# Splitting layer outputs before they are turned, and turning them by DMA: a four-layer graph network on one core

## The reference

```
x = layernorm(x + L0(x));  x = layernorm(x + L1(x));  x = layernorm(x + L2(x));  out = layernorm(x + L3(x))
L0: h = layer_norm(relu(conv(x, W1, b1)), gamma, beta);  conv(h, W2, b2) + x
    conv(x, W, b) = D^-1 H B^-1 H^T (x W^T) + b,  H = (adj != 0), D and B sums over H and the first row of adj
L1: q, k = split(x @ Wqk);  v = x @ Wv
    w = mask * sum(q * (adj @ (k * mask)), features) / 16
    softmax(w over the 64 nodes of a graph) * v
L2: 8 heads of 32: softmax((q k^T / sqrt(32)) * 2 adj) v, then Wo
L3: xg = x * sigmoid(deg * Wd + bd);  s = sigmoid(xg Wqk^T + b);  a = (s s^T / 16) * adj, rows divided by their sums
    relu(a @ xg @ Wl^T + bl + xg @ Wr^T)
```

## Time and profile before

| | us |
|---|---|
| three runs | 959.28, 960.44, 968.0 (median 960.44) |
| span of the profiled execution (first to last instruction) | 966.0 |
| PE / DVE / ACT / POOL busy | 887.1 / 742.3 / 724.6 / 670.3 |
| share of the 16 DMA engines | about 41% |
| pace of a step with all streams live | about 26.5 |

### The profile page before, as it was taken

The page is one execution under the profiler, slowest core; times in us unless marked ns, Lnnn a source line. Parts: engine busy times, 40 slices in busy tenths (PEclk is TensorE's granted clock), DMA queues, the critical chain, the costliest instruction groups (busy, mean ns, idle before and its releaser), DMA issues.

```text
span 966.0 us, 34322 instructions
## 1 busy us (share of the span) xinstructions
PE 887.1 (92%) x12124; PEld 761.5 (79%) x12124; DVE 742.3 (77%) x2292; ACT 724.6 (75%) x1740; POOL 670.3 (69%) x1005
## 2 busy tenths in 40 slices
PE   4778898999999999999999999999999999988674
PEld 3556677888888888888888888888888888876542
DVE  5556776888888888888888888888888888876632
...
PEclk9798899999999999999999999999999999999955
...
GB/s 207 20 21 83 111 100 65 119 111 106 112 123 121 116 116 102 103 112 109 106 109 110 122 123 117 114 106 99 111 119 103 104 115 116 109 97 116 97 48 22
DMA packets 194573, 99.46 MB, mean 103 GB/s; under 512 B 112866, under 2 KB 194276, under 8 KB 194532
## 3 DMA queue, kind: packets, MB, share of 16 engines
...
...
## 4 chain that ended last, share of the span: by engine, by line
PE 53%; ACT 11%; POOL 10%; DVE 10%; issue 9%; DMA 5%; SPq 1%; POOLq 0%; DVEq 0%; ACTq 0%
PE bank L537 12%; PE bank L539 12%; PE bank L538 12%; POOL rFl L1375 3%; PE bank L562 3%; ACT r L886 3%; PE bank L754 2%; PE bank L815 2%; DMA k_by_head<-kst 2%; DMA Ks<-k_by_head 2%; PE bank L650 1%; ACT x L846 1%; PE bank L682 1%; ACT rFh L826 1%; POOL rsC L1391 1%
## 5 line engine op out<-in xcount | busy, mean ns | idle before, releaser
L1375 POOL TENSOR_TENSOR rFl<-r,rFh 128x512 f16<-128x512 f32 x64 | 74.2, 1160 | 81.1 <-ACT rFh L826 81.1
L537 PE MATMUL bank<-z1h,W 128*128 128x256 f16 x256 | 71.9, 281 | 6.3 <-DVE z1l L1025 6.3
L538 PE MATMUL bank<-z1l,W 128*128 128x256 f16 x256 | 71.8, 281 | 0.0
L537 PE MATMUL bank<-W,rFh 128*128 128x256 f16 x256 | 71.8, 280 | 0.0
L539 PE MATMUL bank<-z1h,W 128*128 128x256 f16 x256 | 71.7, 280 | 0.0
L539 PE MATMUL bank<-W,rFl 128*128 128x256 f16 x256 | 71.7, 280 | 0.0
L538 PE MATMUL bank<-W,rFh 128*128 128x256 f16 x256 | 71.7, 280 | 0.0
L1476 POOL TENSOR_TENSOR late<-late,Smx 128x512 f32<-128x512 f32 x64 | 66.8, 1043 | 1.3 <-DVE Smx L1282 1.0
L1375 POOL TENSOR_TENSOR y0l<-y,y0h 128x512 f16<-128x512 f32 x32 | 37.3, 1166 | 42.3 <-ACT y0h L826 42.3
L870 ACT ACTIVATE Pf<-bank,Dinv 128x128 f32<-128x128 f32 x64 | 20.0, 363 | 49.7 <-DVE Dinv L1167 49.7
L886 ACT ACTIVATE r<-bank,b1c 128x256 f32<-128x256 f32 x128 | 50.1, 471 | 4.8 <-PE bank L539 4.8
...
## 6 DMA issues: line engine op xcount, KB each, us to landing
Qs<-q_by_head SPq DMA_DIRECT2D x96, 128.0 KB, 2.7
Ks<-k_by_head SPq DMA_DIRECT2D x96, 128.0 KB, 3.2
Vbd<-vst SPq DMA_DIRECT2D x128, 66.0 KB, 2.1
xin<-x SPq DMA_DIRECT2D x32, 256.0 KB, 2.8
q_by_head<-qst SPq DMA_DIRECT2D x32, 256.0 KB, 2.5
k_by_head<-kst SPq DMA_DIRECT2D x32, 256.0 KB, 2.1
out<-late SPq DMA_DIRECT2D x32, 256.0 KB, 2.9
...
```

The source lines that it names most:

```text
L537: pe.matmul(o, sh, mh, start=start, stop=False, skip_group_check=True)
L538: pe.matmul(o, sh, ml, start=False, stop=False, skip_group_check=True)
L1375: return pool.tensor_tensor(dst, a, b, ALU.subtract)
```

## The change

- **Split before turning.** `x1`, `x2`, `cx`, `xg` and the convolution matrix are cast and subtracted in node-major order into one float16 tile with a high and a low half (`x1s`, `x2s`, `cxs`, `xgs`, `Ps`), and one DMA transpose on SP turns both halves (`x1T`, `x2T`, `cxT`, `xgT`, `Pt`). The PE transposes of these tiles go away. The low parts of `x1` and `cx` are made by POOL, those of `x2`, `xg` and `Ps` by DVE.
- **Layer 1's maximum over a scratch.** The logits `wcol` are written to DRAM (`w_by_node`, a column of single floats) and read back so that each partition has the 64 logits of its graph (`wrow`); DVE takes the maximum of that. Both PE transposes of the logits go away; the sum of the exponentials becomes two float16 matmuls.
- **Two normalizations on VectorE.** `x1` and the output `x4` are made by `tensor_scalar` (subtract, multiply) on DVE, no longer by ACT; POOL's `nb` goes away. The product that makes `xg` moves from POOL to DVE, and ACT's `g2` goes away.
- **Queries stacked later.** `park_q` and `fetch_q` move from `stream2` to `stream3`, one step later.
- Loads: adjacency arrives in the layouts that the tiles need, so `atA`, `aC` and `atG` are one DMA each in place of two, three and two.
- All order tables are new.

```diff
+            def turn(dst, src, done):
+                return sp.dma_start_transpose(dst, src).then_inc(ev(done), 16)
+            def turn_x2(at):
+                sp.wait_ge(ev("x2_lo"), at.n()).then_inc(ev("sp_held"), 1)
+                if at.earlier(1):
+                    sp.wait_ge(ev("v"), at.n(-1)).then_inc(ev("sp_held"), 1)
+                turn(x2T[:].rearrange("p t l c k -> p (t l c) k"), x2s[:].rearrange("p t l d -> p (t l d)"), "x2_turned")
...
+            def park_w(at):
+                sp.wait_ge(ev("w_masked"), at.n()).then_inc(ev("sp_held"), 1)
+                sp.dma_start(w_by_node[at.par].rearrange("t p -> p t"), wcol[:], allow_slow_non_contiguous=True).then_inc(ev("w_parked"), 16)
+            def fetch_w(at):
+                sp.wait_ge(ev("w_parked"), at.chain(16, 16)).then_inc(ev("sp_held"), 1)
+                for b in range(2):
+                    rows = slice(b * NODES, (b + 1) * NODES)
+                    sp.dma_start(wrow[rows], w_by_node[at.par][:, rows].rearrange("(o t) k -> o t k", o=1).broadcast_to(
+                        [NODES, TILES, NODES])).then_inc(ev("w_spread"), 16)
...
             def stream1(at):
-                return
+                turn_x1(at)
                 yield
             def stream2(at):
+                park_w(at)
+                yield
+                fetch_w(at)
+                yield
+                turn_x2(at)
+                yield
+                load_layer2(at)
+                yield
+            def stream3(at):
                 park_q(at)
                 yield
                 fetch_q(at)
                 yield
-                load_layer2(at)
-                yield
-            def stream3(at):
                 park_k(at)
...
             def stream2(at):                                   # PE
-                pe.wait_ge(ev("w_masked"), at.n())
-                pe.transpose(bC[:, 0:P], wpad[:], ident[:]).then_inc(ev("w_turned"), 1)
-                yield
-                pe.wait_ge(ev("w_shifted"), at.n()).then_inc(ev("pe_held"), 1)
-                pe.transpose(bC[:, D:D + P], wrm[:].rearrange("t b k -> t (b k)"), ident[:]).then_inc(ev("w_back"), 1)
...
-                pe.wait_ge(ev("xC"), at.n())
+                pe.wait_ge(ev("x2_turned"), at.chain(16, 16))
                 if at.earlier(1):
                     pe.wait_ge(ev("s_masked"), at.tile(1, -1))
-                turn(bD0, x2).then_inc(ev("x2_turned"), 1)
-                yield
-                first_needs(at, 5)
-                pe.wait_ge(ev("x2F_lo"), at.n())
-                project_fm(bD1, Wq, x2Fh, x2Fl).then_inc(ev("q"), 1)
+                project_turned(bD1, Wq, x2T).then_inc(ev("q"), 1)
...
-                act.wait_ge(ev("x2_turned"), at.n())           # ACT
-                cast(x2Fh[:].rearrange("p c k -> p (c k)"), bD0[:]).then_inc(ev("x2F_hi"), 1)
+                act.wait_ge(ev("xC"), at.n())
+                cast(x2s[:, :, 0], x2[:]).then_inc(ev("x2_hi"), 1)
...
+            def norm(k, dst, at):                              # DVE, for x1 and x4
+                dve.wait_ge(ev("rstd" + k), at.chain(2, 2))
+                for t in range(TILES):
+                    m = dve.tensor_scalar(dst[:, t], pre[k][:, t], mv[k][:, t, 0:1], rs[k][:, t:t + 1], ALU.subtract,
+                                          ALU.mult)
...
-                dve.wait_ge(ev("w_turned"), at.n())
-                dve.tensor_reduce(wmx[:], wv, AX.X, ALU.max).then_inc(ev("c_softmax"), 1)
+                dve.wait_ge(ev("w_spread"), at.chain(32, 32))
+                dve.tensor_reduce(wmx[:], wrow[:], AX.X, ALU.max).then_inc(ev("c_softmax"), 1)
...
-                low(x2Fl[:].rearrange("p c k -> p (c k)"), bD0[:], x2Fh[:].rearrange("p c k -> p (c k)")
-                    ).then_inc(ev("x2F_lo"), 1)
+                dve.tensor_tensor(x2s[:, :, 1], x2[:], x2s[:, :, 0], ALU.subtract).then_inc(ev("x2_lo"), 1)
```

More of the change, by code:

```diff
@@ L84, in build @@
         q_by_head = [nc.dram_tensor(f"q_by_head{i}", (2, P, 2 * TOK), F16).ap() for i in range(2)]
+        w_by_node = [nc.dram_tensor(f"w_by_node{i}", (TILES, P), F32).ap() for i in range(2)]
         k_by_head = [nc.dram_tensor(f"k_by_head{i}", (2, P, 2 * TOK), F16).ap() for i in range(2)]
@@ L372, in load_layer1 @@
                 sp.dma_start(aC[:, at.par], at_group(adj_mask, at)).then_inc(ev(f"C_in{at.par}"), 16)
-                for b in range(2):
-                    sp.dma_start(mrow[64 * b:64 * b + 64, at.par], mr[b, bass.ds(at.group(), 1)].broadcast_to(
-                        [64, TILES, NODES])).then_inc(ev(f"C_in{at.par}"), 16)
             def load_layer2(at):
@@ L385, in load_layer3 @@
                     sp.wait_ge(ev("attn"), at.n(-2)).then_inc(ev("sp_held"), 1)
[L386 to L389 removed]
+                sp.dma_start(atG[:, at.par], at_group(adj_graph, at)).then_inc(ev(f"atG_in{at.par}"), 16)
+            def turn(dst, src, done):
+                return sp.dma_start_transpose(dst, src).then_inc(ev(done), 16)
@@ L616, in stream0 @@
                 yield
-                pe.wait_ge(ev("p_f"), at.n())
-                for t in range(TILES):
-                    m = pe.transpose(bA[:, TOK + t * P:TOK + (t + 1) * P], Pf[:, t], ident[:])
-                m.then_inc(ev("p_turned0"), 1)
-                yield
-                pe.wait_ge(ev("p_lo"), at.n())
+                pe.wait_ge(ev("p_turned"), at.chain(16, 16))
                 pe.wait_ge(ev("x_lo"), at.n())
@@ L976, in stream4 @@
                 yield
-                act.wait_ge(ev("cx_turned"), at.n())
-                cast(cFh[:].rearrange("p c k -> p (c k)"), bF0[:]).then_inc(ev("cF_hi"), 1)
+                act.wait_ge(ev("cx"), at.tile(1))
+                if at.earlier(1):
+                    act.wait_ge(ev("cx_turned"), at.chain(16, 16, -1))
+                cast(cxs[:, :, 0], cx).then_inc(ev("cx_hi"), 1)
                 yield
@@ L1169, in stream0 @@
                 dve.wait_ge(ev("p_hi"), at.n())
-                low(Pl[:, at.par].rearrange("p t k -> p (t k)"), bA[:, TOK:2 * TOK],
-                    Ph[:, at.par].rearrange("p t k -> p (t k)")).then_inc(ev("p_lo"), 1)
+                for t in range(TILES):
+                    m = low(Ps[:, t, 1], bA[:, t * P:(t + 1) * P], Ps[:, t, 0], Dinv[:, t:t + 1])
+                m.then_inc(ev("p_lo"), 1)
                 yield
@@ L1377, in rstd @@
             def rstd(k, at):
-                per = 2 if k in CENTRED else 3
                 eps, factor = {"F": (EPS, 1.0 / (WS * WS)), "G": (EPS * WS * WS, 1.0)}.get(k, (EPS, 1.0))
@@ L1389, in rstd @@
                 yield
-                pool.wait_ge(ev("rstd" + k), at.chain(per, 1))
+                pool.wait_ge(ev("rstd" + k), at.chain(2, 1))
                 pool.tensor_tensor(rs[k][:], ve[k][:], powm[:], ALU.pow).then_inc(ev("rstd" + k), 1)
-                if k in CENTRED:
-                    return
-                yield
-                pool.wait_ge(ev("rstd" + k), at.chain(3, 2)).then_inc(ev("pool_held"), 1)
-                for t in range(TILES):
-                    m = pool.tensor_scalar(nb[k][:, t:t + 1], mv[k][:, t, 0:1], rs[k][:, t:t + 1], -1.0, ALU.mult,
-                                           ALU.mult)
-                m.then_inc(ev("rstd" + k), 1)
             def bias_tm(dst, src, b):
```

338 lines of the change are left out of this document (178 added, 160 removed).

## The result

The changed kernel takes 1358.0 us (median of 4 runs, 1355.5 to 1364.9) beside 959.9 of the kernel before on the same chip: ratio 1.415 [1.407, 1.424], so 398 us slower. The forecast was 988 us, its range 928 to 1042.

A forecast was written before the change was run, and what follows sets the result against it. PE set the pace before; afterwards a loop through SP's transpose of `x2` was to make steps 27.0 us against 26.5. 966.0 + 13 (steps) + 15 (filling, draining) = 994, less 5.6 for the profiled run: 988 us, range 928 to 1042.

The forecast's parts named there:

- What closes the step: Loop through SP's transpose of `x2` and the logits' round trip: (a), (b), 0.1 and (c) make 27.0 us a step.
- (a): Logits' round trip through DRAM, `w_by_node` write (landing 2.1, at most 3.2) and `wrow` reads: 5.45 us.
- (b): DVE's work from `wmx` to `x2_lo`: 10.4 us without waits, 10.9 with one wait for the keys.
- (c): SP's issues and gaps from the transpose of `x2` to the next `w_by_node`: 10.5 us.
- The second loop: From keys landing at 12.85 us through scores, first-layer products, ACT, squares and DVE up to the logits: 27.1 us.
- DVE and POOL: Work per step after the change: DVE about 23.2 us, POOL about 20.5, neither over PE's 23.2.
- Filling and draining: Pipe's start and end, one group 16 us longer at each: +15 us taken, between 0 and 32.
- A: Rival: loop at the transpose of `x2` doesn't close, step 24.2 to 25.4 us, 915 to 946 us; chance 0.20.
- B: Rival: gaps and round trip short, fill and drain partly hidden, step 25.4 to 26.3, 946 to 970 us; chance 0.17.
- C: Rival: DMA rings crowd, round trip and `Ks` land 1 to 2 us later, 1014 to 1053 us; chance 0.13.
- D: Rival: PE's granted clock falls to 0.87, step 28.5 us or more, over 1027 us; chance 0.08.
- What it said the profile would show: Step of 27 us, SP waiting 3 to 4 before transposing `x1` or `x2`, DVE waiting at `wmx`, clock 1.00.

The follow-up runs named there:

- e1: Changed kernel without the logits' DRAM write and both reads, maximum taken over zeros: 1173.0 us, ratio 1.220 to the kernel before.
- e2: Changed kernel with the logits' scratch in node, tile order, so the write is 128 pieces of 8 bytes: 1180.7 us, ratio 1.228.
- e3: Changed kernel with layer 1's maximum found on chip by a DVE diagonal spread and one PE matmul, no DRAM scratch: 1179.6 us, ratio 1.225.
- e5: e1 with three POOL operations (`xl`, `x2b`, `gp`) cut to one column: 1122.4 us, ratio 1.167, step 30.7 us.
- e8: e3 with a new order on all engines, in which POOL also waits until `HBl` is done: 1152.1 us, ratio 1.202, step 31.4 us.
- e7: e1 with 12 idle PE matmuls ahead of each of PE's two long waits: 1163.0 us, ratio 1.209.
- e6: e1 with the convolution matrix `Pf` transposed on PE again, not by DMA: 1175.6 us, ratio 1.222.
- e9: e3 with POOL making `rsq` before `veF`: 1187.6 us, ratio 1.239.
- e13: e3 with PE's product with `Wo` moved ahead of the scores: 1246.8 us, ratio 1.301.
- e16: e3 with `HBl` cut to two columns a tile: 1158.5 us, ratio 1.202.

## Why the prediction was wrong

- **What closes the step: right, with (a) mis-sized.** On the rows of SP and DVE (a), from `w_by_node` to `wmx`, is 650.98 to 664.53, 13.55 us for 5.45; (b), `wmx` to `x2_lo`, 12.1 for 10.9; (c) 11.9 for 10.5. The sum is 37.7 for 27.0, and 8.1 of the 10.7 are (a). There the write was put at 2.1 us, at most 3.2, by rows of 256 and 128 KB; its SP wait alone ends 10.0 after the issue. The prediction named it the step trusted least, and still let large transfers bound it. Its upper end should have come from there being no row at all of such a write.
- **The second loop: failed.** It was to be 27.1 us: 12.85 from the step's beginning, right behind the logits, to the landing of the keys, and 14.2 from there to the next logits. With (a) out of the way (e1, e2, e3) steps are 32.4 to 32.7, and e3's chain holds little of PE:

```profile
DVE 34%; POOL 23%; issue 19%; PE 11%; DMA 5%; SPq 5%; ACT 3%; POOLq 1%; DVEq 0%; ACTq 0%
```

In e3 the two parts are 15.7 and 17.0 us (means of 24 full steps, from `wcol` to the landing of the last `Ks` and on to the next `wcol`). In the first, SP's list was summed as if nothing in it had to wait. SP does wait, before it writes the keys, until DVE has made `kst`, which stands behind the lengthened `HBl` in DVE's order:

```profile
SPq L432 <- DVE kst L1041: 120.7, 31, 4.5
```

That is 3.9 us a step, and it was there before the change with 68.4 us in all. In the second, the sum had 4.7 us for ACT and two squares, and e3's chain runs over POOL alone from 620.6 to 629.9:

```profile
605.98 2.33 DVE HBl L1035 x2
...
614.45 2.55 DMA Ks<-k_by_head
...
622.18 2.28 POOL rFl L1404 x2
```

With POOL's three operations cut (e5) the parts are 13.9 and 16.7; with POOL held off and the new order (e8) 12.7 and 18.6, so there the keys land as forecast and the way back takes what they gained.

- **DVE and POOL: failed.** 23.2 and 20.5 us were costed, 26.8 and 22.7 came. Durations were taken from rows in which the two did not meet; now `HBl` meets `x2b` and `gp`, `HBh` meets `y0l` and `HT` meets `xin`, and the three take 1.4, 0.7 and 0.5 us a step more than before, 2.7 of the 3.6. ACT (19 forecast, though by its own terms, three operations of 0.5 less, it is 20.6; 20.1 measured) and SP's issuing (18.5, 18.5) held, though `Pt` took 1.23, near its upper end, for 0.65.
- **Filling and draining: failed in size.** 26 steps × (38.2 - 26.5) = 304 us; the remaining 94 of 398 lie there, for +15 (0 to 32). Without the round trip (e1) 51 us of them stay, 39 up to the seventh `HT` and 12 behind the last, so not only the logits' 4.6 was too short.
- **The rivals.** A and B (a step shorter than before) are out: even without the round trip it is still 22% slower. C (crowded transfers) was right that transfers hold each other up, but on its own count wrong: it reckoned with about 18 of 27 us, by 1.2 per transpose where its rows give 3.1 - 1.27 = 1.8, and the share is 0.50 to 0.55; `Ks` and `wrow` land in 2.6 and 2.7; it is one small write that stops its neighbours. D (the clock): 0.86 was seen; raising 0.91 to 0.95 (e7) gave nothing clear, and the rest is open.
- **What it said the profile would show.** SP's wait before `x1T` (135.5 us in all) and DVE's before `wmx` (179.3) are there, and the transposes are gone from PE. SP was to wait nowhere else for long, and waits longest for the column (232.3). The clock at 1.00 and the step of 27 are not there either.

Open is most of the 22%: about 50 us go with POOL's three operations (e5); 160 or so could be laid to no one place by e6 to e9 and e13 to e16. No run puts the transposes of `x1`, `x2`, `cx` and `xg`, the largest part of the change, back on PE, so what their landings cost is not measured. That many short handovers between DVE, POOL and SP add up where PE's list was full is argued from the chain, not shown.
